# Causal attention on one core: from image by image to one stream of 128 head pairs, with scaled probabilities and a transposed values product

## What is computed

```
q = h @ w_q / sqrt(128);  kv = h @ w_kv;  k = kv * (1 + k_weights)
logits = q k^T per head, -1e6 above the diagonal
a = softmax(logits);  y = a @ kv
x = x + ga * (y @ w_o)
```

## Time and profile before

| | us |
|---|---|
| median of 3 runs (3782.62 to 3786.3) | 3785.93 |
| the profiled execution, its own time | 3785.41 |
| its span, first to last instruction | 3783.7 |
| TensorE busy in the span | 3158.0 |
| VectorE busy | 2837.6 |
| ScalarE busy | 2301.5 |
| GpSimd busy | 594.3 |

### The profile page before, as it was taken

The page is one execution under the profiler, slowest core; times in us unless marked ns, Lnnn a source line. Parts: engine busy times, 40 slices in busy tenths (PEclk is TensorE's granted clock), DMA queues, the critical chain, the costliest instruction groups (busy, mean ns, idle before and its releaser), DMA issues. The chain is left out here.

```text
span 3783.7 us, 53293 instructions
## 1 busy us (share of the span) xinstructions
PE 3158.0 (83%) x15621; PEld 2172.3 (57%) x15621; DVE 2837.6 (75%) x9954; ACT 2301.5 (61%) x3735; POOL 594.3 (16%) x688
## 2 busy tenths in 40 slices
PE   6999999731525999999999999999999999998564
PEld 5777777620513665565566566565665655665243
DVE  4555555538435898898898898888988988998375
ACT  3444444310214787887888788787887878888310
POOL 0000000010631111111111111111211111211122
PEclk9999999955758999999999999999999999999766
DMA  1000000000421000000000000000000000000000
GB/s 48 0 0 0 0 0 0 1 23 0 106 35 57 1 1 23 7 1 23 7 1 23 7 1 23 7 1 18 12 1 18 12 1 1 1 1 1 6 0 23
DMA packets 30486, 46.51 MB, mean 12 GB/s; under 512 B 4152, under 2 KB 20600, under 8 KB 30240
## 3 DMA queue, kind: packets, MB, share of 16 engines
q1 hardware_dynamic: 24608, 39.47, 3.2%
q0 software_dynamic: 5632, 4.20, 0.8%
HBM read 35.17 MB, written 8.49 MB: 12 GB/s over the span
## 5 line engine op out<-in xcount | busy, mean ns | idle before, releaser
L1684 DVE TENSOR_SCALAR t_feat_q<-t_recip,t_neg_mean 128x256 f32<-128x256 f32 x1024 | 393.7, 446 | 137.7 <-ACT t_recip L1540 130.2
L1387 PE MATMUL t_o_ps<-t_feat_q,t_wo 128*128 128x512 f32 x1024 | 479.5, 601 | 14.4 <-issue 11.8
L1532 ACT ACTIVATE t_recip<-t_feat_q,t_z_scale 128x256 f32<-128x256 f32 x1024 | 434.6, 498 | 1.8 <-DVE t_feat_q L1684 1.0
L1518 ACT ACTIVATE t_exp_k<-t_k_ps 128x1024 f32<-128x1024 f32 x256 | 259.9, 1015 | 250.9 <-PE t_k_ps L1364 250.9
L1647 DVE CUSTOM_DVE_ANT_0 t_junk<-t_v_ps,t_feat_k 128x256 f32<-128x256 f32 x1024 | 391.1, 418 | 23.9 <-PE t_v_ps L1364 23.8
L1637 DVE SCALAR_TENSOR_TENSOR t_feat_k<-t_exp_k,t_k_ps 128x256 f32<-128x256 f32 x1024 | 369.1, 416 | 30.5 <-ACT t_exp_k L1518 30.5
L1522 ACT ACTIVATE t_exp_q<-t_q_ps 128x1024 f32<-128x1024 f32 x256 | 261.7, 1022 | 95.3 <-PE t_q_ps L1364 95.0
L1673 DVE SCALAR_TENSOR_TENSOR t_feat_q<-t_exp_q,t_q_ps 128x1024 f32<-128x1024 f32 x256 | 312.7, 1221 | 8.8
L1387 PEld LDWEIGHTS t_o_ps<-t_feat_q,t_wo 128*128 128x128 f32 x1024 | 195.3, 191 | 191.8 <-issue 171.3
L1362 PE MATMUL t_v_ps<-t_x_hi,t_w_hi 128*128 128x512 f32 x512 | 265.3, 518 | 26.8 <-DVE t_w_lo L1628 17.0
L1540 ACT ACTIVATE t_recip<-t_recip 128x1024 f32<-128x1024 f32 x256 | 269.6, 1054 | 2.7
(11 more groups left out here) (348 smaller groups left out, 7488.8 us busy)
## 6 DMA issues: line engine op xcount, KB each, us to landing
t_raw_w<-in_wk SPq DMA_DIRECT2D x8, 512.0 KB, 3.7
t_raw_w<-in_wq SPq DMA_DIRECT2D x8, 512.0 KB, 4.5
t_raw_w<-in_wv SPq DMA_DIRECT2D x8, 512.0 KB, 5.4
t_raw_o<-in_wo SPq DMA_DIRECT2D x8, 512.0 KB, 3.8
t_raw<-in_w SPq DMA_DIRECT2D x16, 256.0 KB, 2.7
x<-in_x SPq DMA_DIRECT2D x4, 512.0 KB, 7.0
tokens_dram<-r_hn SPq DMA_DIRECT2D x8, 256.0 KB, 2.3
e_w_raw<-in_fc_w SPq DMA_DIRECT2D x4, 512.0 KB, 4.3
```

The lines of the kernel that those rows point to most:

```text
L1387: last = pe.matmul(o_ps[:], wo[:, chunk, :], feat_q[:, s, chunk, :], start=(chunk == 0), stop=(chunk == NC - 1), skip_group_check=True)
L1518: act.activation(exp_k[:], k_ps[:], ACT.Exp, bias=-1.0).then_inc(c["k_exp"], 1)
L1532: last = act.activation(recip[:, q % 2, k * UNIT + n * SEQ:k * UNIT + (n + 1) * SEQ], feat_q[:, s, chunk, cols], ACT.Ln, bias=1.0, scale=z ...
L1684: last = dve.tensor_scalar(feat_q[:, s, chunk, cols], recip[:, q % 2, k * UNIT + n * SEQ:k * UNIT + (n + 1) * SEQ], -1.0, neg_mean[:, s, n ...
```

## The change

All 128 pairs ("units") run through one pipeline that does not stop between images. In step k every engine does a part of several units, in a fixed order:

- TensorE: projections of unit k+1 into the single bank `misc` (q and kv half each), kv turned of unit k into `spare` (half of the `av` bank), probabilities turned of unit k-3, once an image `turn_x` or `turn_o`, logits of unit k, once an image `fill_o`, values product of unit k-4.
- ScalarE: drains q of k+1, kv by token of k, exponentials of k-1 with row sums (`accum_out`), y of k-4, head 1's turned probabilities of k-3.
- VectorE: scales the probabilities of k-2 by the reciprocal sums, drains kv of k+1, head 0's turned probabilities of k-3, maxima of k.

The values product now has `kv_tok` (128 x 64, no ones column) as stationary operand and the turned probabilities (256 columns, then 128) moving. Head 0 writes output partitions 0 to 63, head 1 partitions 64 to 127, of one bank. The result is y transposed, so `turn_y`, the buffer `a_y`, its division and its copies by two engines go; one ScalarE copy is left. The bodies left out of the diff below (modulate, gate_o, split_h, find_moments, normalise, add_x) keep their operations.

```diff
-        kv_tok = sb("a_kv_tok", [P, QT, HEADS, VAL + 1])
-        negmax = sb("a_negmax", [P, HEADS // 2, 4])
-        probs = sb("a_probs", [P, 2, 2, 384])
+        kv_tok = sb("a_kv_tok", [P, QT, NC, P])
+        negmax = sb("a_negmax", [P, PAIRS, 4])
+        probs = sb("a_probs", [P, 4, 2, 384])
+        sums = sb("a_sums", [P, 4, 2, 2])
+        inv = sb("a_inv", [P, 4, 2, 2])
         probs_t = sb("a_probs_t", [P, 2, 2, 384])
-        inv = sb("a_inv", [P, 2, 2, 1])
-        y = sb("a_y", [P, QT, HEADS, VAL])
-        y_t = sb("a_y_t", [P, NC, SEQ])
+        y_t = sb("a_y_t", [P, 2, NC, SEQ])
...
         pair = [ps(f"a_pair{i}", [P, 2, 512]) for i in range(2)]
-        bank = [pair[i // 2][:, i % 2, :] for i in range(4)]
-        turn = [ps(f"a_turn{i}", [P, 512]) for i in range(2)]
-        av = ps("a_av", [P, 2, 2, VAL + 1])
-        misc = ps("a_misc", [P, 512])
...
+        turn = ps("a_turn", [P, 2, 512])
+        av = ps("a_av", [P, 2, SEQ])
+        spare = av[:, 1, :].rearrange("p (i t) -> p i t", i=QT)
+        misc = ps("a_misc", [P, 2, SEQ])
...
+        def run(eng, step):
+
+            for k in range(-8, 8):
+                step(0, k)
+            with eng.Fori(0, BATCH // 2 - 1) as j:
+                for k in range(8, 24):
+                    step(j, k)
+            for k in range(8, 23):
+                step(BATCH // 2 - 1, k)
+
+        def live(j, k):
+
+            return not isinstance(j, int) or 0 <= 2 * PAIRS * j + k < UNITS
+
+        unit = lambda j, k: 2 * PAIRS * j + k
+        image = lambda j, k: 2 * j + k // PAIRS
+        opens = lambda k: k % PAIRS == 0
+        ends = lambda k: k % PAIRS == PAIRS - 1
 
...
+            def drain_q(j, k):
+                act.wait_ge(c["qkv_filled"], unit(j, k) + 2)
+                if unit(0, k) >= PAIRS or not isinstance(j, int) or j:
+                    act.wait_ge(c["logits_ready"], unit(j, k) - PAIRS + 2)
+                at = k % PAIRS
+                act.activation(q_t[:, at, :], misc[:, 0, :], ACT.Copy, scale=g["kw"][:, at:at + 1]).then_inc(c["q_drained"], 1)
+
+            def drain_kvtok(j, k):
+                act.wait_ge(c["kvtok_filled"], unit(j, k) + 2)
+                act.activation(kv_tok[:, :, k % PAIRS, :], spare, ACT.Copy).then_inc(c["kvtok_drained"], 1)
...
+            def drain_probs(j, k):
+                act.wait_ge(c["turned"], unit(j, k) + 2)
+                act.activation(probs_t[:, k % 2, 1, :], turn[:, 1, 0:384], ACT.Copy).then_inc(probs_t_ready[1], 1)
+
+            def exponentials(j, k):
+                s, at = k % 4, k % PAIRS
+                act.wait_ge(c["negmax_ready"], unit(j, k) + 2)
+                for head in range(2):
+                    act.activation(probs[:, s, head, 0:P], pair[k % 2][:, head, 0:P], ACT.Exp, bias=negmax[:, at, head:head + 1],
+                                   accum_out=sums[:, s, 0, head:head + 1])
+                    last = act.activation(probs[:, s, head, P:384], pair[k % 2][:, head, P:384], ACT.Exp,
+                                          bias=negmax[:, at, 2 + head:3 + head], accum_out=sums[:, s, 1, head:head + 1])
+                last.then_inc(c["probs_ready"], 1)
...
+            def drain_y(j, k):
+                act.wait_ge(c["av_ready"], unit(j, k) + 2)
+                act.activation(y_t[:, k // PAIRS % 2, k % PAIRS, :], av[:, 0, :], ACT.Copy).then_inc(c["y_t_ready"], 1)
+
+            def step(j, k):
+                if live(j, k + 1):
+                    drain_q(j, k + 1)
+                if live(j, k):
+                    drain_kvtok(j, k)
+                if live(j, k + 6) and opens(k + 6):
+                    modulate(j, k + 6)
+                if live(j, k - 1):
+                    exponentials(j, k - 1)
+                if live(j, k - 5) and ends(k - 5):
+                    gate_o(j, k - 5)
+                if live(j, k - 4):
+                    drain_y(j, k - 4)
+                if live(j, k - 3):
+                    drain_probs(j, k - 3)
+
+            run(act, step)
 
...
+            def drain_kv(j, k):
+                dve.wait_ge(c["q_drained"], unit(j, k) + 2)
+                if unit(0, k) >= PAIRS or not isinstance(j, int) or j:
+                    dve.wait_ge(c["logits_ready"], unit(j, k) - PAIRS + 2)
+                dve.tensor_copy(kv_t[:, k % PAIRS, :], misc[:, 1, :]).then_inc(c["kv_drained"], 1)
+
+            def scale_probs(j, k):
+                s = k % 4
+                dve.wait_ge(c["probs_ready"], unit(j, k) + 2)
+                dve.reciprocal(inv[:, s, :, :], sums[:, s, :, :]).then_inc(c["inv_ready"], 1)
+                dve.wait_ge(c["inv_ready"], unit(j, k) + 2)
+                for head in range(2):
+                    dve.tensor_scalar(probs[:, s, head, 0:P], probs[:, s, head, 0:P], inv[:, s, 0, head:head + 1], None, ALU.mult)
+                    last = dve.tensor_scalar(probs[:, s, head, P:384], probs[:, s, head, P:384], inv[:, s, 1, head:head + 1], None, ALU.mult)
+                last.then_inc(c["norm_ready"], 1)
...
+            def drain_probs(j, k):
+                dve.wait_ge(c["turned"], unit(j, k) + 2)
+                dve.tensor_copy(probs_t[:, k % 2, 0, :], turn[:, 0, 0:384]).then_inc(probs_t_ready[0], 1)
...
+            def find_max(j, k):
+                at = k % PAIRS
+                dve.wait_ge(c["logits_ready"], unit(j, k) + 2)
+                dve.tensor_reduce(negmax[:, at, 0:2], pair[k % 2][:, :, 0:P], AX.X, ALU.max, negate=True)
+                dve.tensor_reduce(negmax[:, at, 2:4], pair[k % 2][:, :, P:384], AX.X, ALU.max, negate=True).then_inc(c["negmax_ready"], 1)
+
+            def step(j, k):
+                if live(j, k + 6) and opens(k + 6):
+                    normalise(j, k + 6)
+                if live(j, k - 2):
+                    scale_probs(j, k - 2)
+                if live(j, k + 5) and opens(k + 5):
+                    split_h(j, k + 5)
+                if live(j, k + 1):
+                    drain_kv(j, k + 1)
+                if live(j, k - 7) and ends(k - 7):
+                    add_x(j, k - 7)
+                if live(j, k - 3):
+                    drain_probs(j, k - 3)
+                if live(j, k + 8) and opens(k + 8):
+                    find_moments(j, k + 8)
+                if live(j, k):
+                    find_max(j, k)
+
+            run(dve, step)
             dve.wait_ge(c["x_added"], BATCH + 1)
...
+            def fill_qkv(j, k):
+                u, b, chunk, s = unit(j, k), image(j, k), k % PAIRS, k // PAIRS % 2
+                if opens(k):
+                    pe.wait_ge(c["h_split"], b + 2)
+                if chunk == 6 and (not isinstance(b, int) or b >= 1):
+                    pe.wait_ge(c["o_ready"], b + 1)
+                if not isinstance(u, int) or u >= 1:
+                    pe.wait_ge(c["kv_drained"], u + 1)
+                three_pass(misc[:, 0, :], 0, chunk, s)
+                three_pass(misc[:, 1, :], 1, chunk, s).then_inc(c["qkv_filled"], 1)
+
+            def turn_kv(j, k):
+                u, b, chunk = unit(j, k), image(j, k), k % PAIRS
+                pe.wait_ge(c["kv_drained"], u + 2)
+                if not isinstance(u, int) or u >= 1:
+                    pe.wait_ge(c["kvtok_drained"], u + 1)
+                if not isinstance(u, int) or u >= 5:
+                    pe.wait_ge(c["y_t_ready"], u - 3)
+                if chunk == 3 and (not isinstance(b, int) or b < BATCH - 1):
+                    pe.wait_ge(c["h_ready"], b + 3)
+                if chunk == 7 and (not isinstance(b, int) or b >= 1):
+                    pe.wait_ge(c["x_added"], b + 1)
+                for i in range(QT):
+                    last = pe.transpose(spare[:, i, :], kv_t[:, chunk, i * P:(i + 1) * P], g["ident"][:])
+                last.then_inc(c["kvtok_filled"], 1)
...
+
+            def turn_probs(j, k):
+                u, s = unit(j, k), k % 4
+                pe.wait_ge(c["norm_ready"], u + 2)
+                for head in range(2):
+                    if not isinstance(u, int) or u >= 1:
+                        pe.wait_ge(probs_t_ready[head], u + 1)
+                    for m in range(3):
+                        last = pe.transpose(turn[:, head, m * P:(m + 1) * P], probs[:, s, head, m * P:(m + 1) * P], g["ident"][:])
+                last.then_inc(c["turned"], 1)
+
+            def values(j, k):
+                u, b, at = unit(j, k), image(j, k), k % PAIRS
+                for head in range(2):
+                    pe.wait_ge(probs_t_ready[head], u + 2)
+                if not isinstance(u, int) or u >= 1:
+                    pe.wait_ge(c["y_t_ready"], u + 1)
+                pe.wait_ge(c["kvtok_drained"], u + (6 if live(j, k + 4) else 2))
+                if at == 6 and (not isinstance(b, int) or b + 2 < BATCH):
+                    pe.wait_ge(c["h_ready"], b + 4)
+                if at == 2 and (not isinstance(b, int) or b >= 1):
+                    pe.wait_ge(c["x_added"], b + 1)
+                for head in range(2):
```

(141 more changed lines are left out.)

235 lines of the change are left out of this document (50 added, 185 removed).

## The result

| | before | changed |
|---|---|---|
| median of 4 runs | 3786.11 us (3782.62 to 3789.64) | 3651.0 us (3646.99 to 3655.99) |
| ratio | | 0.9639, 95% interval 0.9618 to 0.9661 |
| profiled execution, span | 3785.41, 3783.7 us | 3646.99, 3645.2 us |
| attention, its last instruction's end | 742.85 us | 596.66 us |
| TensorE busy in it | 646.0 of 712 us | 557.2 of 566 us |

The forecast was 3644 us in a range of 3610 to 3722.

What follows compares the result with a forecast made beforehand. TensorE was taken to bound the 712 us attention phase; a new phase of 565 us plus 6 us allowance saves 141 us, so 3785.4 - 141 = 3644 us. Range 3610 to 3722, the forecast's own 3610 to 3680.

Steps and rivals of the forecast that it cites:

- The step: TensorE's work on one unit in the attention: projections, kv and probabilities turned, logits, values product; 3.82 us, eight 30.6.
- The values product: On TensorE, two heads on column halves, priced like the row-halves logits at 0.96 us with drains on both sides.
- An image: TensorE's attention work for one image, eight steps plus once-an-image parts: 34.8 us, 16 images 557.
- the parts once an image: On TensorE, `fill_o` with a slow first slot, `turn_x` and `turn_o` with their waits: together 4.2 us.
- beginning and end: First steps short of work and the last unit's bare chain in the attention: 8 us for both.
- the allowance of 6 us for ScalarE's margins: ScalarE's order in a step leaves 0.2 to 0.4 us, none at the high price; 0.05 us a step allowed.
- bound 509: VectorE's busy time in the new attention: at most 509 us of 565, the scaling hidden behind TensorE.
- Column halves without overlap: Rival in the values product: 1.46 us for 0.96, 64 us more, kernel at 3708; chance 0.13.
- Lock-step of ScalarE and VectorE: Rival: late exponentials and y's copy stop TensorE at `turn_kv`; 0.4 us a step, 51 us, 3695; chance 0.16 together with issue.
- Issue: Rival: seven more semaphore waits a unit on TensorE, 0.05 us each, 45 us, 3689; chance 0.16 together with lock-step.
- The clock in the attention: Rival: TensorE at 1.2 GHz part of the time; at half the stream 280 us more, 3924; chance 0.03.
- nothing else is touched: Outside the attention, 712 of 3783.7 us, the rest of the kernel was taken as unchanged.

Runs made afterwards that it cites:

- Experiment 6: Changed kernel with the pipeline of units filled and drained once an image instead of running through all 128 units; 3757.05 us, ratio 0.993.
- experiment 1: Changed kernel with the values product's four matmuls issued head by head instead of both heads' 256 columns, then both heads' 128; 3654.73 us, ratio 0.9653.
- experiment 2: Changed kernel with the values product on whole columns, head 1 written over head 0, so half of y is left out; 3702.41 us, ratio 0.978.
- experiment 3: Changed kernel with the mask's four products ahead of the logits' own, one change of array shape a step less; 3642.92 us, ratio 0.9619.
- experiment 4: Changed kernel without the softmax division: no row sums, no reciprocal, no scaling; 3630.64 us, ratio 0.9592.
- experiment 5: Changed kernel with the four scaling instructions of each unit standing twice, the first set to an unread tile; 3669.28 us, ratio 0.9693.

## Why the prediction was right

**What bounds the kernel, and why it gets shorter: right.** TensorE bounded the phase and still does. The two sources named, the cheaper step and the closed seams, are both there: 89 us of the gain are busy time, 57 idle time. Experiment 6 weighs them in one order only, the stream last (118 us of 146).

**The step: 3.82 forecast, 3.77 measured.** Projections 0.82 (305.14 to 305.96) for 0.78; kv turned 0.21 for 0.22; probabilities 0.75 with the drain behind them for 0.67 + 0.10; logits 0.33 + 0.53, mask and drain 0.33, together 1.19 (306.92 to 308.11) for 1.09 + 0.10; values 0.80 (308.11 to 308.91) for 0.86. The values product was taken from the row halves of the logits, the nearest row, and this held to 0.06 us. Experiments 1 and 2 show that column halves overlap as row halves do: the Trainium skill, "TensorEngine Tiling (Array Packing)", Key Properties, says that different tiles run in parallel, and the runs agree, 1.28 us for the whole array against 0.80 in halves. The rule of the same section of the Trainium skill, that a change of mode drains the array, agrees too: experiment 3 takes one such change away and gains 0.11 us in an ordinary step.

**An image: 34.8 us forecast, 34.79 measured** (`fill_o` at 323.72, the next at 358.51). That this agrees so well is luck: eight steps came out 0.40 us under the forecast (30.16 for 30.56), the parts once an image 0.43 over (4.63 for 4.2). The step with `fill_o` takes 3.50 us more than an ordinary one for 3.37 forecast, those with `turn_x` and `turn_o` 0.54 and 0.46 more for 0.42 each, and the step behind `turn_x` 0.17 for nothing (together 4.67; a few ordinary steps are 3.74). 16 images are 556.6 us; beginning and end take the other 9.5 of 566.1, forecast at 8. Of the allowance of 6 us for ScalarE's margins about 2.8 were needed, in the one step an image where `modulate` makes ScalarE late (experiment 4); elsewhere ScalarE waits for TensorE at y's copy, 112 times. So the attention was forecast at 571 us with the allowance and took 566.1.

**VectorE: right, with room.** The four scaling instructions take at most 1.07 us (305.59 to 306.66, where the copy of kv starts, just behind ScalarE's of q; in experiment 5 one such set is followed by the next after 0.92), bound 1.54; VectorE is busy 417.7 us, bound 509. Experiment 4 shows them hidden (2.8 us of attention for the whole division), and experiment 5 the depth of the cover: one more set costs 18 us.

**ScalarE: right.** The accumulator reads take 0.09 of the sequence each (307.04 to 307.13), as in the earlier trace rows; busy 413 us for 472. y's copy ends 0.50 into the step (0.6 forecast), the exponentials at 3.37 (3.4).

**Rivals.** Column halves without overlap: refuted by the paired starts of experiment 1 together with experiment 2. Lock-step of ScalarE and VectorE: no idle of TensorE in an ordinary step, 0.17 us once an image, inside the allowance. Issue: none of TensorE's waits in the attention is put down to it. The clock in the attention: granted at 1.00. None of them is in the 7 us by which the forecast fell short.

**What was missed: the term put at zero, "nothing else is touched".** The attention did 5 us better than forecast (146 saved for 141), yet the kernel came out 7 us slower than forecast. The profiled pair shows +5.6 us in the experts, +12.7 in the stack and -9.7 in the last stage, beside -0.9 in the others: 7.7 us more, so that this pair ends some 2.6 us above the forecast. The other 4 are the distance of the profiled run (3646.99) from the median of its four (3651.0). The experts' part is shown: it goes when TensorE's code is shifted, in one profile of each of two shifts.

The other two spread within one and the same kernel, and with the clock. The last stage takes 211.1 us at 0.70 and 220.3 to 220.8 at 0.65 or 0.66. In the stack, the trace's records of the clock add up to 115 us at the 1.2 GHz level before and 135 in the changed kernel; half of the 20 us more is 10 of the 12.7. In all fourteen profiles the stack less half its time at that level is 2346 to 2355 us, though the stack itself spreads from 2398.0 to 2424.1. Why the clock is granted so isn't shown. Whether the stack is on the whole slower behind the new attention stays open, though it looks so: 2398.0 to 2405.6 us in three profiles of before, 2402.3 to 2424.1 in eleven of the new attention, nine of them above all three.

## What to carry to other kernels

Where the bounding engine idles at the ends of a repeated pipeline, multiply one beginning and one end by the number of repeats for a first estimate: 7.6 us by 15 gave 114, and undoing the stream cost 118, though 94 of it was idle time and the rest longer matmuls, which the estimate left out. Such a seam is that of the new pipeline; the old one's is read from its own waits. Price a new kind of matmul by the nearest shape in the trace, count changes of the array's shape (0.1 us each here), and order the work of a step so that like shapes stand side by side. Expect some us of a large gain to move elsewhere: compare the unchanged stages one by one before crediting or blaming an edit, as experiment 4 shows.

## What was unexpected of the hardware

- Two heads' matmuls on different column halves overlap even if issued head by head (0.81 us against 0.80, and the heads' instructions start together in both). My expectation was that they overlap only with their neighbour in the queue.
- Unchanged code of TensorE changes its speed when other code stands ahead of it: 12 gaps, 13.3 us of TensorE and about 6 us of the kernel, gone with 64 or 160 instructions more ahead of it.
- Around the gaps, a packet of the kind "instruction" is missing that all profiles without gaps have (14 profiles).
- From one profile of the same kernel to the next, the last stage takes 211.1 or 220.3 us (the changed kernel, clock 0.70 and 0.66), 214.3 or 220.8 (the kernel before), and the stack differs by up to 8 us (before: 2398.0 and 2405.6).
